# Feed-forward input transposed as pairs of 64-row halves, the second halves of a pair behind a wait on the first

## The reference

```python
x = x + _L0_attn_ref(_layernorm(x), Wq, Wk, Wv, Wo)
x = x + _L0_xattn_ref(_layernorm(x), ctx_1024, pos, pos, Wq, Wkv, Wout, bout)
x = x + _L0_ffn_ref(_layernorm(x), wq_gate, s_gate, wq_up, s_up, wq_down, s_down)
# the feed-forward part, W = (wq - 128) * scale:
gate = silu(x @ Wgate.T)        # 512 -> 1408
up = x @ Wup.T                  # 512 -> 1408
return (gate * up) @ Wdown.T    # 1408 -> 512
```

## Time and profile before

| what | value |
|---|---|
| median of 3 runs | 1677.18 us (1676.98 to 1678.65) |
| the profiled execution's own time | 1680.36 us |
| its span in the trace | 1678.5 us |
| TensorE matmul busy over the span | 1625.0 us (97%) |
| VectorE busy | 1162.9 us (69%) |
| ScalarE busy | 967.3 us (58%) |
| GpSimd busy | 548.4 us (33%) |

### The profile page before, as it was taken

How to read it: one execution, slowest core, us unless ns; L and a number is a source line. 1 busy time by engine, 2 the same in 40 slices (tenths; PEclk the granted TensorE clock), 3 DMA queues, 4 the chain that set the end, 5 groups by cost and what they waited for, 6 DMA issues and landing times. The chain is left out here.

```text
span 1678.5 us, 42062 instructions
## 1 busy us (share of the span) xinstructions
PE 1625.0 (97%) x15216; PEld 1267.4 (76%) x15216; DVE 1162.9 (69%) x2087; ACT 967.3 (58%) x3847; POOL 548.4 (33%) x535
## 2 busy tenths in 40 slices
PE   6899999999999999999999999998999999999997
PEld 4677777777777777777777777766888888888885
DVE  7788788888888888888888878786744344344332
ACT  5577677777777777777767777675422222222221
POOL 4344443444444444444444444341011011011011
PEclk9999999999999999999999999998999999999999
DMA  6011111111110011111111011022420120120110
GB/s 215 29 32 31 36 34 50 30 30 36 41 43 30 30 36 47 37 30 36 30 54 30 30 36 33 23 70 90 150 76 26 50 75 25 50 75 25 50 50 26
DMA packets 55098, 81.00 MB, mean 48 GB/s; under 512 B 4880, under 2 KB 25488, under 8 KB 55056
## 3 DMA queue, kind: packets, MB, share of 16 engines
q1 hardware_dynamic: 55056, 80.43, 14.7%
HBM read 63.63 MB, written 16.78 MB: 48 GB/s over the span
## 5 line engine op out<-in xcount | busy, mean ns | idle before, releaser
L949 ACT ACTIVATE prob<-bank,nmax 128x128 f32<-128x128 f32 x1536 | 539.9, 408 | 155.8 <-DVE nmax L1180 151.7
L949 ACT ACTIVATION_READ_ACCUMULATOR prob<-bank,nmax 128x1 f32 x1536 | 380.7, 248 | 0.0
L1588 PE MATMUL fbank<-shared,piece_hi 128*128 128x512 f32 x1152 | 280.3, 394 | 0.0
L1180 DVE TENSOR_REDUCE nmax<-bank 128x4 f32<-128x512 f32 x376 | 233.5, 683 | 64.8 <-PE bank L536 51.2
L1588 PEld LDWEIGHTS fbank<-shared,piece_hi 128*128 128x128 f32 x1152 | 215.8, 187 | 53.2
L399 POOL TENSOR_TENSOR rope_buf<-rope_buf 128x512 f32<-128x512 f32 x128 | 165.6, 1303 | 159.7 <-DVE rope_buf L1133 159.6
L1740 DVE SCALAR_TENSOR_TENSOR h<-fbank,su_c,sil 128x512 f32<-128x512 f32 x88 | 66.0, 750 | 200.1 <-PE fbank L1588 197.1
L1674 ACT ACTIVATE sil<-fbank,sg_c 128x512 f32<-128x512 f32 x88 | 60.5, 687 | 174.8 <-PE fbank L1588 172.2
L1680 ACT ACTIVATE h_h<-h 128x512 fp32r<-128x512 f32 x88 | 55.6, 632 | 175.1 <-DVE h L1740 175.1
L449 POOL TENSOR_TENSOR cn_l<-cn,cn_h 128x512 fp32r<-128x512 f32 x64 | 82.8, 1294 | 211.9 <-DVE cn L1172 211.9
L512 PE MATMUL bank<-shared,z1T_h 128*128 128x512 f32 x520 | 140.4, 412 | 4.5 <-ACT shared L932 2.6
(11 more groups left out here) (178 smaller groups left out, 3170.2 us busy)
## 6 DMA issues: line engine op xcount, KB each, us to landing
xA<-in_x SPq DMA_DIRECT2D x32, 256.0 KB, 3.1
xB<-in_x SPq DMA_DIRECT2D x32, 256.0 KB, 3.0
x_scratch<-x SPq DMA_DIRECT2D x32, 256.0 KB, 2.0
shared_loaded<-x_scratch SPq DMA_DIRECT2D x8, 1024.0 KB, 7.7
xr<-x_scratch SPq DMA_DIRECT2D x8, 1024.0 KB, 5.7
out<-xr SPq DMA_DIRECT2D x8, 1024.0 KB, 4.3
cx<-in_ctx SPq DMA_DIRECT2D x32, 128.0 KB, 2.2
range_window<-in_wg SPq DMA_DIRECT2D x27, 112.0 KB, 2.0
```

What stands on the lines that cost most here:

```text
L949: last = nc.scalar.activation(prob[:, c, i, :], S[c][:, i * P:(i + 1) * P], ACT.Exp, bias=nmax[:, c, i:i + 1], accum_out=rs[:, h:h + 1])
L1180: nc.vector.tensor_reduce(out=nmax[:, c, :], in_=S[c][:, :].rearrange("p (g k) -> p g k", g=G), op=ALU.max, axis=AX, negate=True).then_inc ...
L1588: last = nc.tensor.matmul(dst[:, :], w[:, k, cols], z[:, k, :], start=(n == 0), stop=(n == len(passes) * KT - 1))
```

## The change

`transpose_tile(k)` and `transpose_tile(k + 1)` become one `transpose_two(k, nb)`: 8 half transposes, a wait, 8 half transposes. `zT_d` is now raised by 2 at the end of the pair, in place of by 1 behind each tile. A semaphore of VectorE's is merged with another, so that two new ones fit.

```diff
-        mv_r, ve_r, rs_r, z_r = sem("f_mean_var_ready"), sem("f_var_eps_ready"), sem("f_rough_rstd_ready"), sem("f_z_ready")
+        mv_r, ve_r, rs_r, z_r = sem("f_mean_var_or_rstd_ready"), sem("f_var_eps_ready"), sem("f_rough_rstd_ready"), sem("f_z_ready")
+        halves_d, gate = sem("f_first_halves_transposed"), sem("f_tensor_gate")
...
-        rstd_r = sem("f_rstd_ready")
...
-            def transpose_tile(k, nx):
-                for s in range(TPB):
-                    last = nc.tensor.transpose(TZ[k][:, s * P:(s + 1) * P], xn[:, s, k * P:(k + 1) * P], ident[:, :])
-                last.then_inc(zT_d, 1)
+            def transpose_two(k, nb):
+
+                for swap in range(2):
+                    if swap:
+                        pe.wait_ge(halves_d, 2 * nb + k // 2 + 1)
+                    pe.sem_inc(gate, 1)
+                    for s in range(TPB):
+                        for half, rows in enumerate((slice(0, P // 2), slice(P // 2, P))):
+                            n = k + (half ^ swap)
+                            last = nc.tensor.transpose(TZ[n][:, s * P + rows.start:s * P + rows.stop],
+                                                       xn[rows, s, n * P:(n + 1) * P], ident[rows, rows])
+                    if swap:
+                        last.then_inc(zT_d, 2)
+                    else:
+                        last.then_inc(halves_d, 1)
...
-                        transpose_tile(0, nx)
-                        transpose_tile(1, nx)
+                        transpose_two(0, nb)
...
-                    transpose_tile(2, nx)
-                    transpose_tile(3, nx)
+                    transpose_two(2, nb)
...
-                dve.wait_ge(mv_r, q + 1)
+                dve.wait_ge(mv_r, 2 * q + 1)
...
-                nc.vector.tensor_tensor(nt[:, 3, :], nt[:, 2, :], r0[:, :], ALU.mult).then_inc(rstd_r, 1)
-                dve.wait_ge(rstd_r, q + 1)
+                nc.vector.tensor_tensor(nt[:, 3, :], nt[:, 2, :], r0[:, :], ALU.mult).then_inc(mv_r, 1)
+                dve.wait_ge(mv_r, 2 * q + 2)
```

## The result

The changed kernel takes 1683.29 us (median of 8 runs, 1680.31 to 1687.3) against 1677.91 us (8 runs, 1676.1 to 1679.67) for the kernel before: a ratio of 1.003, 95% interval 1.0021 to 1.0039. It is slower by about 5 us, and the interval reaches from 3.5 to 6.5. The profiled execution took 1681.92 us, its span is 1680.1.

The account below looks back on a forecast made before the run. TensorE's instructions were taken to bound the feed-forward part; 0.32 + 0.46 + 0.15 + 0.40 + 0.33 = 1.66 us a place against 1.34, times 14, adds 4.5 to 1677.18: 1681.7 us, range 1680.3 to 1684.6.

Parts of the forecast that it names:

- What bounds the part: Feed-forward part: TensorE is busy 70.00 of 70.00 us, so gains or losses at its places go into the total.
- The sum of a place: One group of transposes on TensorE, ordinary matmul to second ordinary matmul behind: 1.66 us against 1.34, 0.32 more.
- The wait: Between the two rounds of halves: TensorE idles 0.15 us after the first round's last half, which takes 0.22.
- The rival that the wait costs nothing: Second round follows the first without a stop: a place costs 1.36 us, total 1677.5; chance 4%.
- The way in: Last ordinary matmul to first half: 0.32 us where 0.23 was the pace; upper bound 0.54, total 1684.8, chance 5%.
- that lower bound: Way into the halves 0.09 us cheaper if the gate instruction costs nothing: 1.3 us off in all, 1680.4.
- The copies: Behind the second place, copies lose 0.24 us against the next block's first matmul: slack 0.82 to about 0.57.
- the rival of the lower clock: Transposes and a stop let TensorE's clock fall behind each place: 13.6 us and more, 1695; chance 1%.
- A rival's sum: Halves side by side, going in and out free: a place of 1.10 us, 0.24 less, total 1673.8; chance 2%.
- The total: Whole kernel: 4.5 us added to the 1677.18 median, 1681.7 us, 0.27% slower.

Follow-up runs that it names:

- Experiment 1: Against the change: upper rows of both tiles go to one bank, lower rows to the other, no wait, copies sort columns; 1677.92 us against 1678.7, ratio 0.9999.
- Experiment 2: Against the kernel before: whole transposes, with only the gate instruction (a semaphore increment on TensorE's queue) added ahead of each eight; one run of 1679.68 us.
- Experiment 3: Against the kernel before: whole transposes, but the second tile of each pair waits for the end of the first; one run of 1681.89 us.
- experiment 5: Against the kernel before: halves by bank without a wait, all four tiles of a block in one place; 1674.07 us against 1678.21, ratio 0.9977.
- experiment 4: Against the change: two matmuls of `down` put between the first and second round of a pair, to cover the wait; one run of 1682.81 us.
- experiment 7: Against the change: waits kept, all four tiles of a block in one place, both first rounds ahead of the two second rounds; one run of 1675.45 us.

## Why the prediction was right

- **What bounds the part.** It said that what a place on TensorE gains or loses goes into the total. The places sum to 4.58 us more and the stretch to 4.50. In experiments 1 to 3 and 5 places and stretch agree within 0.1; in 4 and 7 the stretch is 0.9 and 0.6 longer than the places say, where another engine came close.
- **The sum of a place.** 0.32 + 0.46 + 0.15 + 0.40 + 0.33 = 1.66 was forecast; the trace has 0.33, 0.46, 0.15 to 0.16, 0.39 and 0.34, 1.67. Every term came from a row of the attention with the same form, and kept its size in another part of the kernel.
- **The wait.** It was bounded by a single row, the one turn in which nothing stands between the rounds. The first round of that row ran at a granted clock of 0.53; the 0.15 behind it held at 1.00, in all 14 places. Experiment 3 puts the wait between whole transposes with the same 0.15 behind the last record. Experiment 1 takes it away, and a place gets 0.36 shorter. That is near the 0.37 of the prediction (0.22 for the last half and 0.15), but it is made up otherwise: the step between the rounds falls from 0.38 to 0.06 and not to nothing (0.32), and the slower start of the second round goes too (0.05). The rival that the wait costs nothing is out.
- **The way in.** It was bounded below by a free gate instruction. Experiment 2 shows that the gate is free ahead of whole transposes, and with the gate in place the way into the halves still costs its 0.09. So nothing bears out the cause named with that lower bound, and the value that was kept was right.
- **The copies.** The forecast was 0.24 us of slack lost, from 0.82 to 0.57. The loss is right; both ends are 0.03 to 0.04 too high, since they halve a row of two copies, and the first takes 0.69 of the 1.29 us. The trace has 0.78 and 0.54.
- **The clock.** 1.00 in the stretch, with all the stops, so the rival of the lower clock is out, and the transposes don't hold the clock down. The lower clock by which the two executions differ is in the attention, in the execution of the kernel before.
- **A rival's sum.** The place without a price for going in and out leaves out the 0.03 us from the last transpose to the matmul behind it: 1.13 and not 1.10, near 1674.2. Nothing rests on it here.
- **The total.** +4.5 forecast, 5.4 between the medians, 3.5 to 6.5 by the interval; 1681.7 forecast, 1683.29 measured, inside the range. Of the 1.6 between them 0.7 is the median of before itself, now 1677.91 and not 1677.18. What the rest is stays open: the traces show 4.5 us from the change, and the attention alone, mostly by its clock, moved one execution by 3.4 us. The runs of the changed kernel scatter by 7 us (1680.31 to 1687.3), so that its median came within 1.6 us of the forecast is in part luck. The 4.5 of the stretch is not.

## What to carry to other kernels

Cutting full-height transposes in halves that run side by side takes a third off their steps (0.49 us for 0.76), but it pays only where no wait between rounds stands uncovered, and more than 0.04 us a place only where many halves share one way in and out. Price an uncovered wait as the last record plus 0.15 us from start to start, and the way in and out as 0.35 us around the halves' starts (1.80 - 0.99 - two steps of 0.23) against 0.12 around whole transposes (1.34 - 0.76 - 0.46). Before covering a wait, look for a layout that has none: here each half keeping to its own bank, with the copy putting the columns in order for nothing, gave back everything. Read busy time with care: it fell over the span and rose in the part that changed. And once work is gathered in one place, look at when its results are released against when they are needed.

## What the runs showed of the hardware that I had not expected

A wait that is satisfied in time can still cost. In experiments 4 and 7 the copies that the next block waits for ended about 0.07 us ahead of its first matmul. In the last block that matmul itself came 0.08 us late, 0.15 behind the copies; in the others it started on time, but the second came 0.33 us after it in place of 0.23, in all of them but one of experiment 7. The list of waits shows nothing of this for TensorE's matmuls. For its weight loads it does, in experiment 4 (us in sum, times, longest):

```profile
PEld fbank L1588 <- DVE shared L1753: 1.6, 6, 0.3
```

One such block start: VectorE's copy, the two weight loads, the two matmuls, each from a window of its own:

```profile
1288.22 0.69 DVE L1753 TENSOR_TENSOR shared<-fbank,shared 128x512 fp32r<-128x512 f32 x1 [1.76 <-ACT shared L1688]
...
1288.96 0.19 PEld L1588 LDWEIGHTS fbank<-shared 128*128 128x128 f32 x1 [0.25 <-DVE shared L1753]
...
1289.07 0.19 PEld L1588 LDWEIGHTS fbank<-shared 128*128 128x128 f32 x1
...
1288.98 0.51 PE L1588 MATMUL fbank<-shared 128*128 128x512 f32 x1
...
1289.32 0.40 PE L1588 MATMUL fbank<-shared 128*128 128x512 f32 x1
```

The same load in the kernel before, whose matmul starts at 1290.25:

```profile
1290.02 0.19 PEld L1588 LDWEIGHTS fbank<-shared 128*128 128x128 f32 x1
```

So it is the weight load that waits. Before, it starts 0.23 us ahead of its matmul. In experiment 4 the copy ends at 1288.91, the load starts at 1288.96, and the matmul right behind it, recorded as 0.51 us long where its kind takes 0.39. The next load comes 0.11 us after the late one, and its own matmul 0.25 after that, so the lost time shows only at the second matmul. With the copies 0.30 us ahead (experiment 5) the step was 0.24, with 0.16 (one block of experiment 7) and 0.54 (the change) it was ordinary. So what a copy must be ahead of is the load.

The second step of the way out, 0.33 and not 0.23, has the same picture in the change. These are the loads of the two ordinary matmuls at 1283.67 and 1284.01:

```profile
1283.67 0.19 PEld L1603 LDWEIGHTS fbank<-piece_hi,h_h 128*128 128x128 f32 x1
1283.78 0.19 PEld L1603 LDWEIGHTS fbank<-piece_hi,h_l 128*128 128x128 f32 x1
```

The first load starts with its own matmul, the second 0.11 us later, and the second matmul 0.23 behind its load. What keeps the first load behind halves from starting earlier stays open.
